# An RWKV block with a 32-expert layer on one Trainium2 core: gate products inside the z chain, slot and z buffers doubled, scatters over two rounds, the activation product in PSUM, and more weights split during the last expert

## The reference

```python
xn = layernorm(x)
# attention branch, per batch
prev = concat(xn[:, 1:2], xn[:, :-1]);  xx = prev - xn
r, k, v, g = ((xn + xx * tm_i) @ W_i.T for i in "rkvg")
wkv = scan over t:  out = (a + e^u e^k v) / (b + e^u e^k);  a, b = w a + e^k v, w b + e^k
attn = layernorm((sigmoid(r) * wkv * sigmoid(g)) @ Wo.T) * ln_g + ln_b
# expert branch
z = w_norm * rmsnorm(xn);  probs = softmax(z @ w_router);  4 of 32 experts per token, 256 rows each
y = (silu(z @ w_gate[e]) * (z @ w_up[e])) @ w_down[e]          # F = 352
out = sum of the 4 chosen y by weight
    + sigmoid(z @ w_shared_gate) * (silu(z @ sw_gate) * (z @ sw_up)) @ sw_down   # FS = 1408
result = x + attn + out
```

## Time and profile before

| what | value |
|---|---|
| median of 3 runs | 1733.67 us |
| the profiled execution | 1735.99 us, of which 1734.2 us are the span of the trace |
| granted TensorE clock, mean | 0.991 |
| busy: PE, DVE, ACT, POOL | 1653.1, 1275.4, 661.5, 885.7 us |
| projection stage on PE | 0 to 464 us |
| expert stage | 464 to 903 us |
| output stage, batch 0 | 903 to 1021 us |
| output stage, batches 1 to 7 | 1021 to 1734 us |
| memory read and written | 233.61 and 81.36 MB |

### The profile page before, as it was taken

One profiled execution on the slowest core, in us unless ns is written; L12 is line 12 of the kernel. 1 busy time (PEld: TensorE's weight loads), 2 busy tenths in 40 slices (PEclk: granted clock), 3 DMA queues, 4 the chain that ended last, 5 costly groups with the idle time before them and its releaser, 6 DMA issues.

```text
span 1734.2 us, 26081 instructions
## 1 busy us (share of the span) xinstructions
PE 1653.1 (95%) x8496; PEld 1402.8 (81%) x8496; DVE 1275.4 (74%) x1836; ACT 661.5 (38%) x1093; POOL 885.7 (51%) x733
## 2 busy tenths in 40 slices
PE   5889999998899999999998899999999999999998
PEld 4667777876699999999996688888788888888887
DVE  6999989998455555555559887786787768687776
ACT  4545545453466665666653312121121212112121
POOL 3778878886644444444436645252443524253351
PEclk9999999999999999999999999999999999999999
DMA  4354332433476666666687655465444344433431
GB/s 159 146 194 147 132 136 99 168 146 147 153 256 222 230 241 245 241 228 222 239 273 225 212 204 182 144 203 173 146 155 162 113 144 142 135 121 110 164 104 43
DMA packets 123087, 299.47 MB, mean 173 GB/s; under 512 B 20524, under 2 KB 31788, under 8 KB 118384
## 3 DMA queue, kind: packets, MB, share of 16 engines
q1 hardware_dynamic: 103248, 264.08, 42.9%
q0 software_dynamic: 19456, 33.67, 6.9%
q10 hardware_dynamic: 288, 0.52, 0.1%
HBM read 233.61 MB, written 81.36 MB: 182 GB/s over the span
## 4 chain that ended last, share of the span: by engine, by line
PE 69%; DVE 14%; issue 8%; POOL 4%; DMA 3%; ACT 2%; DVEq 0%; SPq 0%; POOLq 0%; ACTq 0%
PE bank L1930 24%; PE bank L1305 16%; PE bank L1944 12%; PE bank L1332 8%; PE bank L1961 5%; DVE mixf L681 3%; POOL slot_tokens L372 2%; PE bank L1297 2%; PE bank L957 2%; DMA z_rows<-z 1%; POOL mix L358 1%; DVE bank L650 1%; DVE z L629 1%; DVE s_wg L1834 1%; DVE ekv L697 1%
## 5 line engine op out<-in xcount | busy, mean ns | idle before, releaser
L957 PE MATMUL bank<-mix,w 128*128 128x512 f32 x1536 | 369.4, 398 | 27.5 <-DVE sr L702 11.0
L957 PEld LDWEIGHTS bank<-mix,w 128*128 128x128 f32 x1536 | 289.3, 191 | 97.9 <-DVE sr L702 10.6
L1930 PE MATMUL bank<-s_zT,s_wu 128*128 128x512 f32 x1056 | 256.3, 392 | 13.5 <-DVE s_act_g L1739 11.5
L1930 PE MATMUL bank<-s_zT,s_wg 128*128 128x512 f32 x1056 | 254.2, 389 | 0.7 <-ACT s_act_g L1650 0.5
L1944 PE MATMUL bank<-s_wd,s_h 128*128 128x512 f32 x1056 | 253.9, 389 | 0.9 <-DVE s_h L1745 0.9
L1930 PEld LDWEIGHTS bank<-s_zT,s_wu 128*128 128x128 f32 x1056 | 198.7, 189 | 57.9 <-issue 16.8
L1930 PEld LDWEIGHTS bank<-s_zT,s_wg 128*128 128x128 f32 x1056 | 197.9, 188 | 43.1 <-issue 1.5
L1944 PEld LDWEIGHTS bank<-s_wd,s_h 128*128 128x128 f32 x1056 | 198.1, 188 | 42.6 <-issue 1.3
L1126 POOL TENSOR_TENSOR e_wg<-e_g_in,e_wg 128x1408 fp32r<-128x1408 f32 x31 | 100.3, 3236 | 210.4 <-ACT e_wg L1150 210.4
L1562 POOL DMA_INDIRECT s_picked<-y_rows,s_slot x128 | 140.5, 1098 | 84.9 <-DVE s_total L1795 45.2
L358 POOL TENSOR_TENSOR mix<-mixf,mix 128x512 fp32r<-128x512 f32 x116 | 154.8, 1353 | 51.5 <-ACT mix L455 50.5
(11 more groups left out here) (158 smaller groups left out, 2451.9 us busy)
## 6 DMA issues: line engine op xcount, KB each, us to landing
s_wu<-wu_split SPq DMA_DIRECT2D x77, 512.0 KB
e_g_in<-in_w_gate SPq DMA_DIRECT2D x32, 704.0 KB
e_u_in<-in_w_up SPq DMA_DIRECT2D x32, 704.0 KB
e_d_in<-in_w_down SPq DMA_DIRECT2D x32, 512.0 KB
y_rows<-e_y SPq DMA_DIRECT2D x32, 512.0 KB, 2.9
s_zT<-zT_parts SPq DMA_DIRECT2D x16, 1024.0 KB, 7.0
zT_parts<-zT_hi SPq DMA_DIRECT2D x8, 1024.0 KB
zT_parts<-zT_lo SPq DMA_DIRECT2D x8, 1024.0 KB
```

The costliest lines, as they stand in the source:

```text
L957: last = pe.matmul(pj[m][:], w[i][:, w_part, k, m * P:(m + 1) * P], mix[:, i % 2, k, x_part, :], start=(k == 0 and q == 0), stop=(k == KC ...
L1930: last = pe.matmul(into[:], w[:, w_part, k, :], zT[:, x_part, k, :], start=(q == 0 and k == 0), stop=(q == 2 and k == KC - 1))
```

## The change

- **Projection, DVE and ACT.** `make_zT` takes a function `between`, and the products of sigmoid(R) and sigmoid(G) for the banks 0 and 1 (`make_gate(b, 0)` and `(b, 1)`) now stand behind the second `make_zf` and not behind the whole chain; on ACT the two sigmoids stand ahead of `z_hi`. In `tail` the order of DVE is kept.
- **z and slot buffers.** `z` has four buffers and four semaphores (two before); `slot`, `token` and the semaphore `scattered` are doubled, so `assign(b)` waits for the scatters of b-2.
- **Scatters.** Of the 16 scatters of a batch 6 now stand in its own round and 10 in the next (11 and 5 before). In front of G's low parts stand 6 more of the batch before, in front of K's 2 (before: 1 and 4), and behind K's none but the one that follows each. The 16 of batch 0 all go to round 1; `assign(0)` and `count(0)` move there too. The tail puts the last ten of batch 6 between K's and V's low parts of batch 7.
- **Scores of batch 7.** `score(LAST)` moves from between the two pairs of G to the middle of the second pair, `turn_score(LAST)` behind it, to the start of the last round.
- **First expert weights.** The three loads of expert 0 are issued one by one: behind the first pair of V, behind V and behind the first pair of R (before: together, as soon as the scores of batch 7 were done).
- **Output.** `hidden` writes its product to a bank of `ob` for f below 10 (before: over `act_g`), and `hidden_hi` and `hidden_lo` read it there. `ahead`, four more staging buffers, takes the gate pieces 1 to 4 while expert 30 is computed; they are split during expert 31, as are U1 and D1. The look-ahead in the loop is then 5, 2 and 3 pieces for G, U and D.

```diff
-        def scatter(b, first, last):
+        def scatter(b, half, first, last):
...
-                    d["slots"], bass.IndirectOffsetOnAxis(ap=slot[:, at:at + 1], axis=0),
-                    token[:, at // TOPK:at // TOPK + 1], None, bounds_check=SLOTS - 1, oob_is_err=False,
-                ).then_inc(scattered, 16)
+                    d["slots"], bass.IndirectOffsetOnAxis(ap=slot[:, half, at:at + 1], axis=0),
+                    token[:, half, at // TOPK:at // TOPK + 1], None, bounds_check=SLOTS - 1, oob_is_err=False,
+                ).then_inc(scattered[half], 16)
...
+                mix_lo_among(b, R_, b - 1, 1 - half, MORE)
+                scatter(b - 1, 1 - half, MORE + KC, NT * TOPK)
             mix_lo(b, G_)
-            scatter(b, 0, SOME)
-            mix_lo_among(b + 1, K_, b, SOME)
-            scatter(b, SOME + KC, MORE)
+            scatter(b, half, 0, MORE - KC)
+            mix_lo_among(b + 1, K_, b, half, MORE - KC)
+            if tail:
+                scatter(b, half, MORE, NT * TOPK)
...
-            wait(dve, z_stored[j % 2], (b * 2 + j // 2) * 16)
+            wait(dve, z_stored[j], b * 16)
...
-        def make_zT(b, half):
+        def make_zT(b, half, between=lambda: None):
             make_zf(b, half, 0)
             make_zf(b, half, 1)
+            between()
             z_lo(b, 0)
...
-            wait(dve, scattered, b * NT * TOPK * 16)
+            wait(dve, scattered[half], uses * NT * TOPK * 16)
...
-            load(0, 0)
+            sp.wait_ge(shared["v_done"], B * KC - 2)
+            load(0, 0, lambda part: sp.wait_ge(shared["v_done" if part == 1 else "r_done"], B * KC - 2 * (part - 1)))
...
+    def hidden_at(f, i):
+
+        return ob[f % 2][:] if f < NFS - 1 else act_g[:, i, :]
...
+            sp.wait_ge(shared["e_wg_lo"], E - 1)
+            sp.wait_ge(shared["e_wu_lo"], E - 1)
+            for f in range(1, AHEAD + 1):
+                load_piece(G, f)
...
-            dve.tensor_tensor(act_g[:, i, :], act_g[:, i, :], up[:], ALU.mult).then_inc(h_made, 1)
+            dve.tensor_tensor(hidden_at(f, i), act_g[:, i, :], up[:], ALU.mult).then_inc(h_made, 1)
...
-            dve.tensor_tensor(h[:, i, 1, :], act_g[:, i, :], h[:, i, 0, :].bitcast(F32),
+            dve.tensor_tensor(h[:, i, 1, :], hidden_at(f, i), h[:, i, 0, :].bitcast(F32),
                               ALU.subtract).then_inc(h_lo, 1)
```

More of the change, by code:

```diff
@@ L576, in one_round @@
                 keep_score(LAST)
-            else:
+            gate_g(b, 0)
+            gate_g(b, 1)
+            if not tail:
                 for k in range(KC):
                     z_hi(b + 1, k)
-            gate_g(b, 0)
-            gate_g(b, 1)
         def last_round():
@@ L984, in first_round, with one_round @@
             project(0, G_, 1)
-        def one_round(b, half, second=False, tail=False):
+        def one_round(b, half, uses, second=False, tail=False):
             project(b, K_, 0)
+            if second:
+                count(0)
             score(b)
@@ L994, in one_round @@
             project(b, V_, 1)
-            count(b)
+            if not second:
+                count(b)
             turn_xn(b + 1, 2)
@@ L999, in one_round @@
             project(b, R_, 0)
+            if second:
+                count(b)
             project(b, R_, 1)
             project(b, G_, 0)
-            if tail:
-                score(LAST)
-            project(b, G_, 1, {3: lambda: turn_score(LAST)} if tail else {})
+            project(b, G_, 1, {2: lambda: score(LAST)} if tail else {})
         def last_round():
+            turn_score(LAST)
             project(LAST, K_, 0)
@@ L1197, in one_expert @@
             silu(e, 1)
+            if not more:
+                output_early[1]()
             hidden_hi(e, 1)
@@ L1433, in zero, with staged @@
         return isinstance(b, int) and b == 0
+    def hidden_at(f, i):
+        return ob[f % 2][:] if f < NFS - 1 else act_g[:, i, :]
+    def staged(which, f):
+        if which == G and 1 <= f <= AHEAD:
+            return ahead[:, f - 1, :]
+        return piece[:, which, :]
     def chunk(t, f):
```

207 lines of the change are left out of this document (121 added, 86 removed).

## The result

| | before | after |
|---|---|---|
| device time, median of 6 runs | 1733.47 us | 1741.53 us |
| lowest to highest | 1731.81 to 1736.81 | 1738.77 to 1743.05 |
| profiled execution; its span | 1735.99; 1734.2 us | 1743.00; 1741.2 us |

The changed kernel is slower: ratio 1.0045, 95% interval [1.0033, 1.0057]. The forecast was 1706.2 us, in a range of 1696 to 1720. Run again beside other kernels the unaltered changed kernel gave 1.0031 [1.0019, 1.0043], so by the medians the loss is 4 to 8 us (1738.32 against 1734.36 in that run) where 27.5 of gain were forecast.

What follows compares the result with a forecast made beforehand. It took PE, busy for most of the span, as what counts, standing still mainly for DVE and POOL. Gains of 1.5 + 9.5 + 3.0 + 13.5 = 27.5 us took the median from 1733.67 to 1706.2 us, range 1696 to 1720.

Steps and rivals of the forecast that it cites:

- Rounds 2 to 5: Projection, 142 to 352 us: gate products come earlier, so K stops waiting for DVE; gain 9.5 us, bounds 0 and 13.
- 6.8 us out of a chain: Rounds 2 to 5, logits to gate products: two z buffer waits and the rest of the z chain go.
- Rival 2: Output batch 0: POOL holds DVE's next two-input instruction instead, only 6.2 us of gate parts saved; 1713.5 us, chance 0.12.
- The 0.5 us a round charged for POOL: Rounds 2 to 5: allowance for G's low parts having no margin behind five more scatters; bounds 0 and 3.
- rival 3: Rounds 1 to 6 and tail: scatters in a row stall POOL ahead of low parts; slower, 1751 us, chance 0.04.
- Rounds 0 and 1: Projection to 142 us: slow first K pair and count wait go, mostly returning as waits; gain 1.5 us, bounds -2 and 7.
- the 10.8 us of both: Round 1: time saved at the K pair and count, expected back as waits at G and the turn of scores.
- Round 6 and the last round: Projection, 352 to 464 us: V starts later but the first expert turn comes earlier; gain 3.0 us, bounds -3 and 6.
- The 5.94 us stall: POOL behind batch 7's first scatter, blamed on expert 0's weights loading in one go; taken as gone, bounds 0 and 5.94.
- Output batch 0: Output stage, first product to Wo: DVE makes hidden earlier; gain 13.5 us, bounds 7 and 17, to about 90.6 us.
- Two terms: Output batch 0 on DVE: hidden_lo freed of POOL's blocking, 5.3 us; four gate parts leave the round, 6.2 us.
- The pieces' waits: Output batch 0: gate parts' waits for high parts shrink by 3 us, as pieces 5 to 10 load five ahead.

Runs made afterwards that it cites:

- e9: Kernel before with four z buffers and a semaphore for each, nothing else of the change; ratio 0.9981 to the kernel before.
- e11: Kernel before with only the doubled slots and moved scatters, batch 0's routing in round 1; ratio 1.0099 to the kernel before.
- e3: Changed kernel with the first expert's three weight loads issued together again, without pacing; ratio 1.0026 to the kernel before.
- e10: Kernel before with four z buffers and the gate products inside the z chain, scatters in their old places; ratio 0.9967 to the kernel before.
- e2: Kernel before with the output stage's part of the change alone; ratio 1.0002 to the kernel before.
- e7: e3 with the last batch's scores ahead of G's second half again; ratio 1.0021 to the kernel before.
- e13: e3 with batch 0's count, assignment and first six scatters back in round 0; ratio 1.0007 to the kernel before.
- e6: e3 with DVE's copies of slots and record moved behind the next batch's K mixes; ratio 1.0027 to the kernel before.
- e17: The changed kernel run once more, unaltered; ratio 1.0031 to the kernel before.
- e16: e10 with the first expert's weight loads paced as in the changed kernel; ratio 0.9977 to the kernel before.
- e15: e2 with the hidden product in SBUF as before, not in PSUM; ratio 1.0006 to the kernel before.
- e5: e3 with four of the six scatters ahead of POOL's G low parts placed among them; ratio 1.0022 to the kernel before.
- e12: e3 with DVE computing only 32 of 512 columns of the z rows of batches 2 to 7; ratio 0.9957 to the kernel before.

## Why the prediction was wrong, step by step

**Rounds 2 to 5, the step that failed.** The chain from the logits to the gate products was worked out with the durations that DVE's instructions had, and then POOL was asked whether it fitted. What POOL's run would do to DVE in its new place was not put on the chain. POOL's own part came out well: its run of G's low parts was forecast at +36.3 us behind the K start and stands at +36.1 in round 3 (228.65, with the K start put 5.6 us ahead of the score at 198.15). But DVE is held to the end of that run, so the gate products start 47.2 to 50.1 us behind the K start and not 43.9.

K no longer waits for them, as said; G's second half waits instead, for the sigmoid behind K's first mix. Behind the two longer of these waits, 2.27 and 2.70 us, 48 matmuls took 13.1 us and not 11.5, at a granted clock of 0.75 and then 0.67 on the mean of 3 us each from 238.1 on, between its two levels of 1.2 and 2.4 GHz; behind the wait of 1.43 us it was 1.00, the upper one.

The round's length did not move: 207.4 to 208.3 us for the four against 206.6 to 210.4, not 200.9. The prediction took 6.8 us out of a chain in an engine that had 9 us of 228 left. e9, with nothing but the z buffers, shows where the waits for z stores went (6.5 us over the window): DVE is busy for 217.0 us and the rounds take 207.8. They were filled with held time.

**The blocking was seen and booked in one place.** Rival 2 (blocking moves to the next two-input instruction) was named for output batch 0 alone, at 0.12 and 0.05, with 7 us at stake. In the projection stage something like it came in every round, and it caught instructions that the prediction hadn't thought of, of 4 and 16 columns. The 0.5 us a round charged for POOL (up to 3 if it met DVE) looked at the wrong victim: the scatters ahead of G's low parts did not make these late for PE (at most one wait of 0.7 us for POOL in rounds 2 to 5); they moved POOL's run of four onto `assign`. That is the slower side that rival 3 should have been: not a stall of scatters in a row, for those of rounds 1 to 6 follow one another at 0.30 us. Measured, the moved scatters cost 17.2 us by themselves (e11), and e3 lies 0.0059, 10 us, above e10, which keeps them in place; the output part and the place of the last scores differ there too, but brought nothing in e2 and e7. Why they cost more alone is open.

**Rounds 0 and 1.** Forecast -1.5, measured within 1.5 us of nothing. The paced K pair and the wait for the count went, as said. In their place PE waits 7.35 us at the turn of the scores of batch 1 and 3.03 at G, where the forecast had the 10.8 us of both come back. The timeline of DVE shows the reason for the first: `assign(0)` stands ahead of V's mixes, which then meet POOL; in e13, with `assign(0)` back in round 0, that wait is 0.50 us.

```profile
88.26 6.63 DVE L684 SCALAR_TENSOR_TENSOR mixf<-xx,keep_const,xnT 128x512 f32<-128x512 f32 x4
```

That the size was about right is luck, for the trade was the wrong one: e10 gets `score(2)` at 140.6 without it.

**Round 6 and the last round.** Forecast V's start 72.9 us behind the K start; by the same mark, `score(6)`, it came 425.15 - 355.22 = 69.9 us later, against 422.73 - 357.92 = 64.8 before: 5.1 more, where 2.5 were allowed. The two further scatters cost about what was said: POOL's first K low part of batch 7 starts at 400.01, as before (400.06), and V's come 2.4 us later, for 2.7 forecast. The rest is the 2.7 us by which the round had begun earlier, and they went in one instruction, DVE ahead of POOL in round 6:

```profile
384.83 5.75 DVE L769 COPY keep_slot<-slot 128x16 uint32<-128x16 uint32 x1
```

```profile
385.50 5.04 POOL L358 TENSOR_TENSOR mix<-mixf,mix 128x512 fp32r<-128x512 f32 x4
```

DVE reached this copy 5.6 us ahead of the kernel before (384.83 against 390.44) and the z chain of batch 7 at 392.98, against 393.02: the lead was gone in the copy. Moving the copy away does not bring it back. In e6 four shift differences take 8.07 us in its place, the z chain starts 37.7 us behind `score(6)` as here (37.8), and V 70.2 us behind it. The 5.94 us stall of the earlier trace rows shrank to 2.25. It is 0.31 in e17, with the loads paced, and 0.30 in e3, where they go out in one go again; on the old order it is 2.93 in e16 with the pacing and 5.06 in e10 without. So the cause that I gave it is not borne out as the whole, and it stays open.

**Output batch 0.** Forecast 90.6 us, measured 104.6. DVE groups, 909 to 1014 us, to be held against the earlier trace rows:

```profile
L1861 DVE SCALAR_TENSOR_TENSOR s_total<-s_picked,s_rec,s_total 128x512 f32<-128x512 f32 x16 | 20.6, 1285 | 0.8
...
L1900 DVE TENSOR_TENSOR s_wg<-s_piece,s_wg 128x512 fp32r<-128x512 f32 x6 | 9.7, 1609 | 5.6 <-issue 4.5 <-ACT s_wg L1750 1.1
...
L1811 DVE TENSOR_TENSOR s_h<-bank,s_h 128x512 fp32r<-128x512 f32 x10 | 6.9, 692 | 7.5 <-ACT s_h L1712 6.2 <-issue 1.3
L1805 DVE TENSOR_TENSOR bank<-s_act_g,bank 128x512 f32<-128x512 f32 x10 | 6.8, 683 | 3.1 <-PE bank L1999 3.1
...
L1851 DVE TENSOR_TENSOR s_gate<-s_gate,s_ek 128x512 f32<-128x512 f32 x4 | 6.0, 1507 | 0.0
```

Two terms came about as forecast: `hidden_lo` 12.2 to 6.9 us, all ten at 0.69, and the gate parts, 15.5 to 9.7 (5.8 for 6.2). The Trainium skill, "SBUF — State Buffer", section "Who interferes with whom", says that a DVE instruction with at most one SBUF input, outside the two-port modes, does not contend with GpSimd, and this row agrees. (One SBUF input alone did not free an instruction in these runs: the copy of the slots has one and was held for 5.47 us.) The row sums `s_total` grew from 16.6 to 20.6 us and the gate product from 4.9 to 6.0. That looks like rival 2, but they are as long in e15 (20.5 and 6.0), where `hidden_lo` is held again, so the bank did not cause it; what did is open. And DVE's idle time grew: busy 86.8 of 105 us against 92.0 of 104. The pieces' waits, which were to shrink by 3 us, are 5.6 against 5.7; one of 4.5 us is the fifth gate piece, whose load stands in SP's queue behind a down piece (issued 913.20) that waits for POOL's low part of piece 1 (909.63 to 913.17). 11.1 us less of two instructions did not make `hidden` earlier. Which of held time and late pieces bounds it was not tried apart; e15 shows only that the product in PSUM brought nothing that could be told.

**The experts and the later output batches** held: no gap, nothing to gain.

**The range.** The lower bounds of its four gains, -2, 0, -3 and 7, add up to a gain of 2 us, so no mix of them could give a loss, and the chance for slower, 0.04, hung on one mechanism that the trace spoke against. No bound had DVE held in the rounds by more than 3 us each, and none had the moved scatters cost more than the other parts bring.

## What to carry to other kernels

Before a wait is taken off a chain, lay the other engine's runs over it in their new places, and where a run meets an instruction that it can hold, take the run's end and not the instruction's own length. Add up the engine's busy time and its waits over one round as well: if they fill it, there is little to gain unless work goes. In these kernels splitting GpSimd's run (e5) or moving the held instruction (e6) moved the loss to the next one, and the edit that shortened rounds 2 to 5 was less work on DVE (e12); less work on GpSimd was not tried. Test the parts of a bundled change apart: here one part lost 17 us alone and the z buffers gained 3. And look at a second profile before explaining a wait that one execution shows.

## What the runs showed of the hardware

In these kernels a DVE instruction was held over a whole run of GpSimd tensor operations that follow without a gap, not over one of them: a copy of 16 columns took 5.47 us beside four operations that took 5.04, and 5.75 beside four more. That it is four in a row and not one is more than I had allowed. When scatters stood between the four (e5), a cast and a product in `assign` took 1.87 to 2.00 us each in every round, none of its instructions took longer, and DVE's busy time was the same. The held kinds in these runs: copy, cast, scalar operations and products of 4 and 16 columns, mixes, z rows, shift differences. The reduction `chosen` took 1.12 to 1.14 us on the mean in every kernel.
